# The third pass's forty block sums on GpSimd instead of VectorE

## What is computed

```python
w = jnp.einsum('bpf,mf->bpm', features, W_ft) + b_ft   # 1024 x 2 x 5128 by 512 x 5128
accumulator = stm * w
l1_x = jnp.clip(accumulator, 0.0, 1.0).reshape(features.shape[0], -1)
l2_x = jnp.clip(l1_x @ W1.T + b1, 0.0, 1.0)
return l2_x @ W2.T + b2
```

## Time and profile before

| What | us |
|---|---|
| time of the kernel, median of three runs | 398.27 (397.55 to 398.43) |
| span of the profiled execution, first to last instruction | 396.4 |
| PE busy | 392.8 |
| DVE busy | 346.9 |
| ACT busy | 197.6 |
| POOL busy | 14.7 |

### The profile page before, as it was taken

One profiled execution on the slowest core, in us unless ns is written; L12 is line 12 of the kernel. 1 busy time (PEld: TensorE's weight loads), 2 busy tenths in 40 slices (PEclk: granted clock), 3 DMA queues, 4 the chain that ended last, 5 costly groups with the idle time before them and its releaser, 6 DMA issues.

```text
span 396.4 us, 4869 instructions
## 1 busy us (share of the span) xinstructions
PE 392.8 (99%) x1862; PEld 323.7 (82%) x1862; DVE 346.9 (88%) x347; ACT 197.6 (50%) x207; POOL 14.7 (4%) x34
## 2 busy tenths in 40 slices
PE   8999999999999999999999999999999999999997
PEld 6888888888888888888888888888788888878886
DVE  3999999999999999999997789999787754999624
ACT  5565556633484434444334864344433447863500
POOL 0000034041000000000000000000000000000000
PEclk9999999999999999999999999999999999999999
DMA  8999979989976677666607689887667778774000
GB/s 271 394 398 400 383 247 362 342 256 230 327 255 233 237 254 263 243 220 235 233 0 256 225 317 397 327 308 236 203 233 257 241 217 247 245 246 132 0 2 3
DMA packets 30775, 97.85 MB, mean 247 GB/s; under 512 B 4024, under 2 KB 10176, under 8 KB 25312
## 3 DMA queue, kind: packets, MB, share of 16 engines
q1 hardware_dynamic: 29392, 95.18, 69.0%
q0 software_dynamic: 1072, 2.10, 1.7%
q10 hardware_dynamic: 288, 0.26, 0.2%
HBM read 96.87 MB, written 0.00 MB: 244 GB/s over the span
## 4 chain that ended last, share of the span: by engine, by line
PE 99%; DVE 0%; issue 0%; DVEq 0%
PE sums L595 94%; PE sums L672 3%; PE sums L711 1%; PE sums L698 1%; PE sums L688 0%; PE sums L706 0%; DVE res L528 0%; DVE hid L522 0%; DVE idle L531 0%; DVEq L527 0%
## 5 line engine op out<-in xcount | busy, mean ns | idle before, releaser
L595 PE MATMUL sums<-x_hi,w_hi 128*128 128x512 f32 x544 | 167.2, 391 | 0.0
L595 PE MATMUL sums<-x_hi,w_lo 128*128 128x512 f32 x544 | 166.5, 389 | 0.0
L595 PEld LDWEIGHTS sums<-x_hi,w_hi 128*128 128x128 f32 x544 | 102.1, 188 | 21.9 <-issue 0.7
L595 PEld LDWEIGHTS sums<-x_hi,w_lo 128*128 128x128 f32 x544 | 102.4, 188 | 21.3
L595 PE MATMUL sums<-x_lo_home,w_hi 128*128 128x512 f32 x384 | 118.4, 389 | 0.0
L355 ACT ACTIVATE x_hi<-xs 128x2048 fp32r<-128x2048 f32 x58 | 110.7, 1908 | 2.2 <-DVE xs L490 1.8
L350 ACT ACTIVATE w_hi<-ws 128x512 fp32r<-128x512 f32 x58 | 36.9, 636 | 147.1 <-PE sums L595 139.0
L499 DVE TENSOR_TENSOR x_lo_home<-xs,x_hi 128x2048 fp32r<-128x2048 f32 x40 | 91.3, 2283 | 12.3 <-ACT x_hi L355 12.3
L595 PEld LDWEIGHTS sums<-x_lo_home,w_hi 128*128 128x128 f32 x384 | 72.1, 188 | 15.0
L483 DVE TENSOR_TENSOR xs<-xs 128x2048 f32<-128x2048 f32 x20 | 45.6, 2281 | 0.7 <-DMA xs<-x_p 0.7
L496 DVE TENSOR_TENSOR w_lo<-ws,w_hi 128x512 fp32r<-128x512 f32 x58 | 39.6, 683 | 6.2 <-ACT w_hi L350 6.1
(11 more groups left out here) (72 smaller groups left out, 199.5 us busy)
## 6 DMA issues: line engine op xcount, KB each, us to landing
xs<-x_p SPq DMA_DIRECT2D x40, 1024.0 KB, 5.7
xs<-x_p SPq DMA_DIRECT2D x56, 512.0 KB, 6.4
ws<-w_p SPq DMA_DIRECT2D x56, 256.0 KB, 3.5
ws<-w_p SPq DMA_DIRECT2D x44, 128.0 KB, 4.7
open_x<-x_p SPq DMA_DIRECT2D x3, 512.0 KB, 6.2
xr_raw<-x_rest POOLq DMA_DIRECT2D x1, 1024.0 KB, 8.5
stm_all<-stm SPq DMA_DIRECT2D x1, 1024.0 KB, 7.6
open_x<-x_p SPq DMA_DIRECT2D x2, 256.0 KB, 4.3
```

Source lines behind the costliest of these rows:

```text
L595: return nc.tensor.matmul(sums[:, bank, :], w[:, m * P:(m + 1) * P], x[:, c * BANK:(c + 1) * BANK], start=start, stop=stop, skip_group_che ...
```

## The change

The forty sums of the third pass, lines 487 and 490, leave DVE's sums_of and are written on GpSimd with the same operands, in the order of the steps, behind GpSimd's last DMA. GpSimd waits once for the kept blocks (s_kept) and for all earlier sums (w_sum and x_sum, so that the counts stay in order), and then, for every sum, for the load of its block alone. DVE's sums_of does nothing for the third pass, and its wait for the W load there is gone.

```diff
             for q in range(R, P, 2 * R):
                 pool.dma_start(xr[q:q + R, :, :].bitcast(F32), xr_low[q:q + R, :, :].bitcast(F32))\
                     .then_inc(rest_ready, 16)
+            pool.wait_ge(s_kept, K_PAIRS)
+            pool.wait_ge(w_sum, TURN)
+            pool.wait_ge(x_sum, x_sums(TURN - 1))
+            for g in range(TURN, TURN + K_PAIRS):
+                k = g - TURN
+                i, j, n = raw_w(g), raw_x(g), slot(g)
+                pool.wait_ge(w_loaded[n], w_count(g))
+                nc.gpsimd.tensor_tensor(ws[:, i + 1, :], ws[:, i + 1, :], ws[:, KEPT + k, :], ALU.subtract)\
+                    .then_inc(w_sum, 1)
+                pool.wait_ge(x_loaded[n], x_count(g))
+                nc.gpsimd.tensor_tensor(xs[:, j + 1, :], xs[:, j + 1, :], xs[:, TST + k, :], ALU.subtract)\
+                    .then_inc(x_sum, 1)
...
-                dve.wait_ge(w_loaded[n], w_count(g))
+                if f < 2:
+                    dve.wait_ge(w_loaded[n], w_count(g))
...
-                elif f == 2:
-                    dve.wait_ge(s_kept, K_PAIRS)
-                    nc.vector.tensor_tensor(ws[:, i + 1, :], ws[:, i + 1, :], ws[:, KEPT + k, :], ALU.subtract)\
-                        .then_inc(w_sum, 1)
-                    dve.wait_ge(x_loaded[n], x_count(g))
-                    nc.vector.tensor_tensor(xs[:, j + 1, :], xs[:, j + 1, :], xs[:, TST + k, :], ALU.subtract)\
-                        .then_inc(x_sum, 1)
```

## The result

The changed kernel takes 409.37 us (408.15 to 410.86, four runs), against 398.35 us before on the same chip: 11.0 us more, a ratio of 1.0278 with a 95% interval of 1.0249 to 1.0306. The profiled run is the fastest of the four (408.15 us); it has a span of 406.3 us, 9.9 us more than before.

A forecast was written before the change was run, and what follows sets the result against it. PE was taken to bound the kernel. With GpSimd and DVE excluding each other, 212.65 + 50.4 + 4.9 + 61.2 = 329.1 against 312.6 gave 16.5 us, so 398.27 + 16.5 = 414.8 us, range 397.6 to 425.4.

The forecast's parts named there:

- PE bounds the pass, DVE's 32.8 us are worth nothing: Third pass: PE has no gap, so the 32.8 us of sums taken off DVE lie beside its work and win 0.
- GpSimd alone keeps up: Third pass: a W and X pair, 2.86 us on GpSimd (1.64 to 3.39), fits the 5.44 us step and is hidden.
- handover: Third pass: 0.1 us added to each GpSimd sum for taking turns with DVE, making a pair 3.06 us.
- Exclusion: Third pass: GpSimd and DVE subtractions never run together, so their work adds up; 16.5 us slower, 414.8 us, chance 0.58.
- The size, 16.5 against 11.0 us: Step 56: both engines' work end to end finishes at 329.1, its low part due at 312.6, so 16.5 us late.
- The point that decides: Step 56's low part sets the loss, late by 16.5 us; after it GpSimd is done and DVE keeps up.
- the delay fits too: Each step: load and X sum take 8 us, while ACT wants X 16.3 us after the load went out.
- The clock: Whole kernel: whether the granted clock stays 1.0 once PE waits was not covered; a fall would put time above the range.
- full overlap: Third pass rival: GpSimd's sums run beside DVE's work and are hidden; 398.3 us, chance 0.36 for full or sufficient overlap.
- partial overlap: Third pass: if some 0.6 us of a step's 6.03 us runs side by side, it fits 5.44 us; 398.3 us.
- GpSimd too slow by itself: Third pass rival: a pair above 5.44 us loses the excess each step; 417 us at 6.78, chance 0.04.
- SP's queue: Load of step 45 waits for step 43's X sum, ending about 232.5 against 232.9 before, so leaves no later.

The follow-up runs named there:

- e3: The changed kernel with DVE's four additions moved from steps 45, 46, 48, 49 to steps 56 to 59; 402.04 us, ratio 1.0094 to the kernel before.
- e9: The changed kernel with the sums of steps 40 and 41 back on DVE and all four additions behind step 59's low part; 398.28 us, ratio 1.0008.
- e4: The changed kernel with each of GpSimd's forty sums replaced by a memset that reads nothing from SBUF; 398.39 us, ratio 1.0005 to the kernel before.
- e6: The changed kernel with DVE's third-pass low parts formed from one operand, high part times a constant; 398.94 us, ratio 1.0027 to the kernel before.
- e10: The changed kernel with only the sums of steps 50 to 59 on GpSimd, additions at their old place; 399.70 us, ratio 1.0037 to the kernel before.
- e1: The changed kernel with only the twenty W sums on GpSimd, the X sums back on DVE; 398.88 us, ratio 1.0008 to the kernel before.
- e2: The changed kernel with only the twenty X sums on GpSimd, the W sums back on DVE; 406.79 us, ratio 1.0213 to the kernel before.

## Why the prediction was right, and where it was off

- **PE bounds the pass, DVE's 32.8 us are worth nothing**: right as far as it could be seen. With as many as 36 sums off DVE and no collision that matters, the time is that of before (398.28 against 398.18), not below it.
- **GpSimd alone keeps up**: right for the pace, wrong for the first steps of the pass (see the entry below). The sums that waited for nothing took 0.74 and 2.39 us (rows at 216.23 and 213.05 in the block below), 3.13 a pair against 5.44 a step; the price taken, 2.86 without handover, was 9% low. To DVE's 1.219 us the X sum is 1.96, the very ratio of the Trainium skill's "GPSIMD Engine Reference", section "Performance versus the Vector engine".

```profile
213.05 2.39 POOL L322 TENSOR_TENSOR xs<-xs 128x1024 f32<-128x1024 f32 x1 [0.20 <-DMA xs<-x_p]
216.23 0.74 POOL L319 TENSOR_TENSOR ws<-ws 128x256 f32<-128x256 f32 x1 [0.79 <-DMA ws<-w_p]
```

- **Exclusion**: right, and shown: by the rows in turns, by e3 and e9 (DVE work that GpSimd does not touch decides the time), and by e4 (without reads it is gone). The Trainium skill's "SBUF — State Buffer", section "Who interferes with whom", said so, and the trace agrees: the second one waits for the whole of the first (4.48 us for a low part of 2.15), and a GpSimd instruction that only writes doesn't take part.
- **The size, 16.5 against 11.0 us**: the term that was mis-sized is the turn. I charged pair and low step 3.06 + 2.97 = 6.03 us; measured is 5.55. There is no handover to pay; on the contrary, in turns each instruction is about 0.14 us shorter than alone (the pair 2.84 instead of 3.13, the low step 2.71 instead of 2.97). That a part of it runs beside its neighbour would explain this; no run tests it. With 2.84, 2.71 and 1.09 for an addition, and this run's own start (212.25) and due time (312.2), the sum of the prediction gives 212.25 + 17 x 2.71 + 4 x 1.09 + 20 x 2.84 - 312.2 = 7.3 us at step 56. The trace has the low part of step 56 done at 320.03, 7.8 after its due time. That they agree so well is in part luck: the X sum of step 59, 2.25 us, came only after that low part, while at the start of the pass neither engine worked for 1.9 us in all, as GpSimd waited for loads and DVE for ACT.
- **The point that decides**: wrong. It was not step 56, at the end of a lag that grows evenly, but steps 47 and 50, right behind the additions. At 5.55 us a step the turns cost 0.11 us a step, which the slack of 5 us takes (e9: nothing). The four additions, 4.4 us of DVE's turns within five steps, are what it could not take, and moving them takes away 7.3 us (e3). So the change got slower by the mechanism that I named, but 11.0 us is not the lateness that I summed up; and the range, from no change to +27.1 us, was so wide that falling inside it says little.
- **The entry**: wrong in "the delay fits too". I took the load of every step to go out when step g - 6 is finished, 16.3 us ahead of ACT. For steps 40 to 43 it goes out only when step g - 4 is finished: that of step 40 left at 207.88, and ACT wanted it at 213.32, 5.44 us later. The 8 us for load and sum do not fit into that. ACT waited 1.9 and 3.0 us for the X sums of steps 40 and 41 ahead of drain(1), and PE then for a bank. The X sum of step 40 ran at its own length (2.39 us, at 213.05), so here GpSimd's sum is late in itself, as the rival of the experiments has it. In the profiled runs PE lost 1.3 us by it in the changed kernel, and about 4.0 us in e3, half clock included.
- **The clock**: named as not covered, it did fall, to half for some 3 us behind the 3.2 us wait, worth about 1.6 us. The entry and the clock are PE's own time, which the sum has no term for: PE began step 56 at 322.13, 2.1 us after its low part was ready, so the end was no longer set there.
- **The rivals**: full overlap is out. The partial overlap was nearer than I had it: pair and low step alone are 3.13 + 2.97 = 6.10 us and take 5.55 in turns, so 0.55 us is saved, where 0.66 would have fitted them into 5.44. The 0.11 us a step that is left is what the slack takes in e9. GpSimd too slow by itself is out for the pass as a whole. What I noted under SP's queue, that the load of step 45 leaves no later, held: 232.38 against 232.92.

## What to carry to other kernels

Work that is moved from VectorE to GpSimd is not taken off VectorE where their instructions exclude each other. Here that held between GpSimd's subtractions or copies out of SBUF and VectorE's fp32 instructions with two inputs, and between GpSimd's subtractions and VectorE's one-input instruction of e6; GpSimd's memset was free of it (e4), and other kinds were not run. In such a case, add both engines' times end to end, step by step, and compare that with the pace of the engine that bounds the pass. Look then for the steps in which the first engine has extra work, since the mean may fit (5.55 against 5.44 us, with slack) where five steps do not; putting that work behind the shared stretch took back most of the loss. Look also for steps whose load leaves later than the others', as at the entry here. And where the bounding engine has no gap, as PE here, such a move has nothing to win.

## What the runs showed of the hardware that I had not expected

- The profile's lengths of VectorE and GpSimd instructions include the wait for the other engine: their rows overlap in time while the work does not (4.48 us for 2.15 us of work, 2.78 for 0.6).
- In the stretches shown, with work queued on both engines, the turns alternate and cost no handover: 0.6 + 0.55 + 2.25 + 2.15 us make up a step of 5.55. That is not so everywhere. GpSimd's first sum in e10 stood behind three VectorE instructions in a row, each at its own length, and its row is 4.90 us long (0.6 us of work); the first W sum of e1 is another, 4.73 us. What decides the order was not tested.

```profile
260.16 4.90 POOL L319 TENSOR_TENSOR ws<-ws 128x256 f32<-128x256 f32 x1 [169.43 <-DVE xs L503]
```

- The granted clock fell to half (1.2 GHz) behind a wait of PE of 3.2 us in the changed kernel, and not behind one of 2.3 us at 289.02 in the same run, where the stretches show 1.00. The length of the one wait does not decide alone: in e3 the clock fell behind a wait of 2.0 us and in e2 behind one of 1.9. What else does stays open.
